# A gated-delta-rule sequence kernel on one core: the order of masks, value convolutions and triangular solves around the end of an iteration

## What is computed

```
mixed = hidden @ W_qkv.T                 # 2048 channels: 512 queries, 512 keys, 1024 values
mixed = silu(causal_conv(mixed, 4 taps)) # each channel by itself
beta  = sigmoid(hidden @ W_b.T);  g = -exp(A_log) * softplus(hidden @ W_a.T + dt_bias)
for t in tokens:                         # 16 heads of 64, state S is 64 x 64
    S = S * exp(g_t);  delta = (v_t - S^T k_t) * beta_t
    S = S + k_t delta^T;  o_t = S^T q_t
out = (rmsnorm(o * silu(hidden @ W_z.T)) * norm_weight) @ W_out.T
```

## Time and profile before

| | us |
|---|---|
| median of 3 runs (lowest, highest) | 1509.21 (1507.35, 1512.29) |
| the profiled execution's own time | 1500.96 |
| its span | 1499.0 |
| PE busy in the span | 1280.1 |
| DVE busy | 908.4 |
| ACT busy | 702.4 |
| POOL busy | 313.7 |

### The profile page before, as it was taken

The page is one execution under the profiler, slowest core; times in us unless marked ns, Lnnn a source line. Parts: engine busy times, 40 slices in busy tenths (PEclk is TensorE's granted clock), DMA queues, the critical chain, the costliest instruction groups (busy, mean ns, idle before and its releaser), DMA issues.

```text
span 1499.0 us, 26935 instructions
## 1 busy us (share of the span) xinstructions
PE 1280.1 (85%) x11040; PEld 926.5 (62%) x11048; DVE 908.4 (61%) x2349; ACT 702.4 (47%) x1353; POOL 313.7 (21%) x234
## 2 busy tenths in 40 slices
PE   3668799788879888889986859998899989989898
PEld 2355668567566766767765536665567656666566
DVE  4897987988798887969155333543436423463321
ACT  1657365564746556482451324424452344523442
POOL 5122352515235151523320010000100000000000
PEclk9768978796897889787898788999999999999999
DMA  4000000000000000010220000000000000000000
GB/s 126 4 2 5 1 2 11 2 12 2 11 1 2 12 2 8 2 33 8 74 86 8 1 1 0 1 8 2 8 0 8 1 2 8 0 1 1 1 8 7
DMA packets 15066, 17.69 MB, mean 12 GB/s; under 512 B 2567, under 2 KB 13216, under 8 KB 14560
## 3 DMA queue, kind: packets, MB, share of 16 engines
q1 hardware_dynamic: 12768, 14.09, 2.9%
q0 software_dynamic: 576, 1.76, 0.4%
q10 hardware_dynamic: 1600, 0.12, 0.1%
HBM read 13.87 MB, written 2.10 MB: 11 GB/s over the span
## 4 chain that ended last, share of the span: by engine, by line
PE 60%; DVE 24%; ACT 10%; issue 3%; POOL 2%; DMA 1%; SPq 0%; DVEq 0%; ACTq 0%
PE ps L1564 8%; PE ps L1554 8%; PE ps L1352 6%; DVE arena L1905 4%; PE ps L1118 4%; PE ps L1262 3%; DVE arena L1908 3%; PE ps L1194 3%; ACT arena L1003 2%; DVE arena L2177 2%; PE ps L1249 2%; PE ps L1656 2%; PE ps L1103 2%; PE ps L1620 2%; DVE arena L1822 2%
## 5 line engine op out<-in xcount | busy, mean ns | idle before, releaser
L1822 DVE SCALAR_TENSOR_TENSOR arena<-ps,conv_w,arena 128x255 f32<-128x255 f32 (+2 forms) x384 | 163.3, 475 | 16.4 <-ACT arena L671 11.8
L965 ACT ACTIVATE arena<-ps 128x512 f32<-128x512 f32 x144 | 85.3, 597 | 180.6 <-PE ps L1554 180.6
L537 POOL TENSOR_TENSOR rstd<-var_eps,half_power 128x2 f32<-128x2 f32 (+1 forms) x28 | 23.3, 834 | 608.7 <-DVE var_eps L1793 608.6
L1564 PEld LDWEIGHTS ps<-arena 128*128 128x128 f32 x1152 | 132.6, 192 | 24.8 <-issue 9.9
L1564 PE MATMUL ps<-arena 128*128 128x128 f32 x1152 | 136.9, 277 | 7.1 <-ACT arena L965 4.1
L1554 PE MATMUL ps<-arena 128*128 128x512 f32 x288 | 134.2, 612 | 0.0
L2148 DVE SCALAR_TENSOR_TENSOR arena<-ps,gates,arena 128x128 f32<-128x128 f32 x128 | 36.0, 343 | 113.8 <-PE ps L1564 113.5
L531 POOL TENSOR_SCALAR arena<-arena 32x1024 f32<-32x1024 f32 x32 | 88.5, 2765 | 53.4 <-DVE arena L1917 51.4
L1905 DVE TENSOR_TENSOR arena<-arena 128x30 f32<-128x30 f32 (+14 forms) x240 | 95.2, 396 | 7.3
L2214 DVE TENSOR_REDUCE arena<-ps 128x8 f32<-128x2048 f32 (+1 forms) x24 | 54.8, 2292 | 63.1 <-PE ps L1620 63.1
L1554 PEld LDWEIGHTS ps<-arena 128*128 128x128 f32 x288 | 51.4, 194 | 60.9 <-issue 45.2
(11 more groups left out here) (246 smaller groups left out, 2830.3 us busy)
## 6 DMA issues: line engine op xcount, KB each, us to landing
arena<-in_routed_up SPq DMA_DIRECT2D x1, 2048.0 KB, 10.2
arena<-in_routed_down SPq DMA_DIRECT2D x1, 2048.0 KB, 14.7
x_ln<-in_x SPq DMA_DIRECT2D x8, 128.0 KB, 2.3
arena<-in_w_mix SPq DMA_DIRECT2D x1, 1024.0 KB, 11.0
x_in<-in_x SPq DMA_DIRECT2D x8, 128.0 KB, 2.4
out_x<-x_res SPq DMA_DIRECT2D x8, 128.0 KB, 1.9
arena<-out_x SPq DMA_DIRECT2D x4, 256.0 KB, 2.8
out_x<-arena SPq DMA_DIRECT2D x4, 256.0 KB, 2.2
```

Of the source, the lines that this page charges most:

```text
L965: act.activation(hid1[half][:, i, :], ps[:, banks[i], :], ACT.Gelu).then_inc(s["mgelu"], 1)
L1564: mm = pe.matmul(ps[:, bank, c * P:(c + 1) * P], hid1[half][:, i, c * P:(c + 1) * P], m_down[:, e, i, :], start=(i == 0), stop=(i == HT1 - 1))
L1822: ins = dve.scalar_tensor_tensor(conv_tile(f, m)[:, sh:SEQ], ps[:, PAIR_BANK[p], j * SEQ:(j + 1) * SEQ - sh], conv_w[:, m, TAPS - 1 - sh:T ...
```

## The change

The pairs 5, 6 and 7 move from banks 4, 2, 4 to banks 1, 2, 2, so that banks 3 and 4 are free once queries and keys are convolved. Batches 0 and 1 both use the first couple of banks of `KK_BANKS` and batch 2 the second (`pair_of`). Products 0, 1 and 2 move on DVE from the start of the next iteration to between the convolutions of the values: pairs 0 to 5, product 0, pair 6, products 1 and 2, pair 7. With them move the keys, sums, decays and silus on PE and ACT, and masks 0 and 1 on POOL ahead of unit blocks 2 and 3. In the next iteration `turn_norm` and `beta_decay` come later on PE, and DVE's remaining products 3 to 7 are spread between the parts of `prepare`, `exponents` and `log_decays`. No instruction is added or taken away. In order on PE, from `solve32` on: sum 0, merge32 twice, pair 5, solve64 twice, first solve_and_merge64, key 0, second solve_and_merge64, pair 6, merge64, sum 1, key 1, merge64, sum 2, pair 7, key 2.

```diff
...
 INV_STEPS = 2 * BLOCK - 2
-PAIR_BANK = (0, 1, 3, 4, 2, 4, 2, 4)
+PAIR_BANK = (0, 1, 3, 4, 2, 1, 2, 2)
...
+def pair_of(k):
+    return max(k - 1, 0) % 2
 def over_heads(ap, n):
...
             normalise(i, 1)
-        if has_n:
-            pool.wait_ge(s["gm_ready"], CH * NB * (n + 1))
+        if has_f:
+            masked_decays(f, 0)
+            masked_decays(f, 1)
+        if has_n:
+            pool.wait_ge(s["gm_ready"], CH * NB * (n + 1) + (2 if has_f else 0))
             after(pool, "hn_ready", CH * (i + 1))
...
             pool.wait_ge(s["ln_rstd"], 1)
-        if has_f:
-            masked_decays(f, 0)
-            masked_decays(f, 1)
-            pool.wait_ge(s["gm_ready"], CH * NB * f + 2)
         if has_n:
...
         i, n, f = it, it + 1, it + 2
-        if has_f:
-            turned_norm(f)
         if has_n:
...
             turned_heads(i - 1, 1, 0)
-        if has_f:
-            exponentials(f)
         if has_n:
             decay_matrix(n, 4)
+        if has_f:
+            turned_norm(f)
         if has_i and i > 0:
...
             decay_matrix(n, 5)
+        if has_f:
+            exponentials(f)
+        if has_n:
             chunk_ends(n)
...
             merged32(n, 0)
+        if has_f:
+            silu(f, 0)
+        if has_n:
             merged32(n, 1)
             solved64(n, 0, 0)
+        if has_f:
+            seed(f, 5)
+            silu(f, 1)
+        if has_n:
             solved64(n, 0, 1)
...
         if has_f:
-            seed(f, 5)
+            silu(f, 2)
+            silu(f, 3)
         if has_n:
...
         if has_f:
-            seed(f, 6)
-            silu(f, 0)
+            decay_matrix(f, 0)
         if has_n:
...
         if has_f:
-            seed(f, 7)
-            silu(f, 1)
+            seed(f, 6)
         if has_n:
...
         if has_f:
-            silu(f, 2)
+            decay_matrix(f, 1)
         if has_n:
...
         if has_f:
-            silu(f, 3)
-            decay_matrix(f, 0)
-            decay_matrix(f, 1)
             decay_matrix(f, 2)
+            seed(f, 7)
     turned_heads(SEQS - 1, 1, 0)
...
         pe.wait_ge(s["d_h_ready"], f + 1)
-        after(pe, "conv_done", NP * f - 1)
+        after(pe, "conv_done", NP * f)
         for c in range(CH):
...
         if p >= 5:
-            pe.wait_ge(s["conv_done"], NP * f + p - 1)
+            pe.wait_ge(s["conv_done"], NP * f + (1, 4, 6)[p - 5] + 1)
         elif not has_n:
...
-            pe.wait_ge(s["conv_done"], NP * n + k + 1)
+            pe.wait_ge(s["conv_done"], NP * n + (0, 5)[k] + 1)
         else:
...
             pe.wait_ge(s["qk_silu"], QK_TILES * (n + 1))
-            pe.wait_ge(s["conv_done"], NP * (n + 1))
-        elif k == 1:
+        elif k == 2:
...
-            pe.wait_ge(s["pt_ready"], CH * NB * n + k - 1)
+            pe.wait_ge(s["pt_ready"], CH * NB * n + max(k - 1, 1))
         for g in range(2):
             r = DH * g
-            mm = pe.matmul(ps[:, KK_BANKS[k % 2][g], 0:2 * P].rearrange("p (q n) -> p q n", q=2),
+            mm = pe.matmul(ps[:, KK_BANKS[pair_of(k)][g], 0:2 * P].rearrange("p (q n) -> p q n", q=2),
                            mix_qk[n % 2][r:r + DH, QK_TILES + b, cs], mix_qk[n % 2][r:r + DH, b::QK_TILES, cs],
...
         i, n, f = it, it + 1, it + 2
-        if has_f:
-            turn_norm(f)
         if has_n:
             decay_sums(n, 3)
-        if has_f:
-            beta_decay(f)
         if has_i and i > 0:
...
         if has_n:
+            key_products(n, 3)
             decay_sums(n, 4)
-            key_products(n, 3)
+        if has_f:
+            turn_norm(f)
         if has_i and i > 0:
...
         if has_n:
+            key_products(n, 4)
+        if has_f:
+            beta_decay(f)
+        if has_n:
             decay_sums(n, 5)
-            key_products(n, 4)
+            key_products(n, 5)
             chunk_ends(n, f, has_f)
             decay_sums(n, 6)
-            key_products(n, 5)
             decay_sums(n, 7)
...
             solve32(i, n, 1, has_i)
+        if has_f:
+            decay_sums(f, 0)
+        if has_n:
             merge32(n, 0)
             merge32(n, 1)
+        if has_f:
+            project(f, 5, n, has_n)
+        if has_n:
             solve64(i, n, 0, has_i)
...
             turn_first(0)
-        if has_f:
-            decay_sums(f, 0)
-            project(f, 5, n, has_n)
         if has_n:
             solve_and_merge64(n, 0)
+        if has_f:
+            key_products(f, 0)
         if it == SEQS - 2:
...
             up_tile(0, 0)
-        if has_f:
-            decay_sums(f, 1)
+        if has_n:
+            solve_and_merge64(n, 1)
+        if has_f:
             project(f, 6, n, has_n)
-        if has_n:
-            solve_and_merge64(n, 1)
         if it == SEQS - 2:
...
             up_tile(0, 1)
-        if has_f:
-            project(f, 7, n, has_n)
         if has_n:
             merge64(n, 0)
+        if has_f:
+            decay_sums(f, 1)
+            key_products(f, 1)
         if it == SEQS - 2:
...
         if has_f:
-            key_products(f, 0)
-            key_products(f, 1)
             decay_sums(f, 2)
+            project(f, 7, n, has_n)
             key_products(f, 2)
...
         dve.wait_ge(s["dm_ready"], CH * NB * n + k + 1)
-        if k == 0:
-            after(dve, "a64_psum", 4 * n)
-        lo, hi = KK_BANKS[k % 2]
+        if b == 0:
+            after(dve, "a64_psum", 4 * (n - 1) + 2 * (c + 1))
+        lo, hi = KK_BANKS[pair_of(k)]
         qk = ps[:, lo:hi + 1, 0:2 * P].rearrange("p g (q n) -> p g q n", q=2)
...
         if has_n:
-            products(me, n, 0)
+            products(me, n, 3)
         if has_f:
...
         if has_n:
-            products(me, n, 1)
-            products(me, n, 2)
+            products(me, n, 4)
         if has_f:
...
         if has_n:
-            products(me, n, 3)
+            products(me, n, 5)
         if has_f:
...
         if has_n:
-            products(me, n, 4)
+            products(me, n, 6)
         if has_f:
...
         if has_n:
-            products(me, n, 5)
+            products(me, n, 7)
         if has_f:
             log_decays(me, f, 2)
-        if has_n:
-            products(me, n, 6)
-            products(me, n, 7)
         if it == SEQS - 1:
...
         if has_f:
-            for p in range(2, NP):
+            for p in range(2, 6):
                 convolve(me, f, p)
+            products(me, f, 0)
+            convolve(me, f, 6)
+            products(me, f, 1)
+            products(me, f, 2)
+            convolve(me, f, 7)
     residual(SEQS - 1, 1)
...
```

More of the change, by code:

```diff
@@ L1460, in _ @@
                     up_tile(0, 0)
-                if has_f:
-                    decay_sums(f, 1)
-                    project(f, 6, n, has_n)
                 if has_n:
                     solve_and_merge64(n, 1)
+                if has_f:
+                    project(f, 6, n, has_n)
                 if it == SEQS - 2:
```

## The result

| | before | changed |
|---|---|---|
| median, us | 1508.28 | 1566.28 |
| ratio to before, 95% interval | | 1.040 [1.0364, 1.0436] |
| span of the profiled execution | 1499.0 | 1561.7 |
| DVE busy | 908.4 | 915.9 |
| PE's granted clock, mean | 0.891 | 0.867 |

A forecast was written before the change was run, and what follows sets the result against it. DVE, spine of a chain through all engines, was taken to bound the kernel by its waits between pair 0 and the inverse: 10.0 us against 7.03, +2.9 per stretch, +17.4 over six, total +17.6, so 1526 us, range 1500 to 1540.

The forecast's parts named there:

- First step: PE from pair 0's convolution: sum 0 waits for it, with all solves queued behind; net delay about 2 us.
- Second and third: DVE among the value convolutions: product 0 waits 3.5 us for decay 0, pair 6 0.75, product 2 1.5 for key 2.
- Fourth: Next iteration: turn_norm waits for prepare, key 4 queued behind; products 4, 5, 6 wait 1.85, 0.75, 1.15 us.
- Rival (c): PE idle 3.2 us ahead of turn_norm drops its clock to half for work behind; +24, 1533 us, chance 0.23.
- Rival (a): Decay 0 is ready when pair 5 ends, so waits shrink; iteration 2.2 us shorter, 1496 us, chance 0.17.
- Rival (b): DVE's waits are moved, not made; iteration within 0.7 us of before, say 1510 us, chance 0.18.

The follow-up runs named there:

- e6_decay0_late: e5_prepare_sum0 with decay 0 moved behind seed 6 on ACT and product 0 behind pair 6 on DVE: 1530.72 us, ratio 1.0177.
- e3_warm: The changed kernel with four added matmuls per iteration on PE ahead of turn_norm, results overwritten: 1539.62 us, ratio 1.0239.
- e1_sum0_late: The changed kernel with sum 0 put back behind the two merge32 on PE: 1552.44 us, ratio 1.0325.
- e4_prepare_early: The changed kernel with the next sequence's two prepare parts moved among the convolutions, ahead of products 0 and 1: 1520.24 us, ratio 1.0099.
- e5_prepare_sum0: The changed kernel with the edits of e4_prepare_early and e1_sum0_late together: 1492.95 us, ratio 0.9912.
- e2_masks_first: The changed kernel with masks 5 to 7 made ahead of the inverse root of the norm on POOL: 1557.07 us, ratio 1.0361.

## Why the prediction was wrong in size

**The bound and the view were right.** DVE is the spine and the loss is DVE's waiting in the stretch from pair 0 to the inverse. The places of the waits were the ones forecast. The times, for T = 398.02, in us after T:

| start of | forecast | measured | behind by |
|---|---|---|---|
| product 0 | 19.55 | 21.0 | 1.4 |
| product 2 | 26.85 | 28.3 | 1.5 |
| turn_norm | 33.4 | 36.0 | 2.6 |
| product 4 | 35.15 | 38.8 | 3.6 |
| product 5 | 37.9 | 43.1 | 5.2 |
| product 6 | 41.1 | 46.6 | 5.5 |
| inverse | 47.5 | 53.0 | 5.5 |

**First step: right in kind, short by 1.4.** Sum 0 waited for pair 0 and all solves moved. The prediction took half clock only "up to T + 13.6", as before; it lasted to T + 18.8, so key 0 and the first solve_and_merge64 had half the speed that I gave them.

**Second and third: right.** DVE waited 4.3 us for decay 0 where I had 3.5, 0.6 for seed 6 (0.75), 1.55 for key 2 (1.5). A reading that came later, in the expectation for e6_decay0_late, that decay 0 was too early on ACT, fell with that run.

**Fourth: this is the step that failed.** It priced PE behind `turn_norm` at full clock: turned heads, key 4, `beta_decay`, sum 5 and key 5 ran at a granted clock of 0.50. Between `turn_norm` and product 5 the measured times fall back by another 2.6 us (2.6 behind, then 5.2), and the waits at products 4 and 5 are 2.80 and 2.62 us where the step had 1.85 and 0.75. The idle time ahead of `turn_norm` was forecast at 3.2 us and measured 4.34. e3_warm shows that this clock is worth 27 us, nearly half of the 58.

Rival (c) had this mechanism, with a chance of 0.23, and its price for it in the stretch, 6.6 - 3.8 = 2.8 us, was about right. Its 50.4 fell short of the 53.6 measured because it kept the other terms of the forecast, and its 40.85 for the inverse that follows because it took for granted that a fall in one stretch spares the next. The kernel before did that by turns; in the changed one no inverse took less than 42.0, and their mean is 43.6.

**What was missing altogether:** the h_tok instructions, 0.59 us for the pair before and 1.78 here. I costed `prepare` at its old duration in a new neighbourhood. In the table that is the step from 1.5 to 2.6 us behind. So of the 5.5 us of this stretch 1.5 come from the half clock in the first step, 1.1 from h_tok and 2.9 from behind `turn_norm`.

**The sum.** It was one iteration's order, worked out at the old clock, times six: +2.9 us a stretch where +9.0 was measured, and nothing for the inverses, which grew by 0.9 each. The repairs of e1_sum0_late and e4_prepare_early take 14 and 46 us off, and both keep the change's idea: masks between the convolutions, the values through banks 1 and 2. The largest single loss was `prepare` behind pair 7 with `turn_norm` needing it, an order that the fourth step names and priced too low. Rival (a), that the overlap works, is out for this order. Its 1496 is close to the 1493 of e5_prepare_sum0, but that is no support for it: it wanted 2.2 us off an iteration by shorter waits in the stretch, and there only 0.3 came off, the rest in the inverses. Rival (b) is out by the interval.

## What to carry to other kernels

A price taken from a stretch holds only with the clock and the neighbours that the stretch had. Where a reordering leaves PE idle for some us, price the work behind the gap at half clock as the first case, and test it by filling the gap with matmuls that nobody reads. When a stage is moved, look at what then precedes it in a queue that must not run dry: here moving 1.5 us of normalisation to a better place gave 46. And where added matmuls raise the clock in one stretch, look for the half clock in the next before counting the gain.

## What the runs showed of the hardware

DVE's normalisation of 128x128 fp32 (SBUF to SBUF, two scalars per partition) takes 0.34 us, and 0.78 and 1.08 beside POOL's 128x512 products. One such case, from the timeline of the changed kernel:
```profile
431.88 1.03 POOL L506 TENSOR_TENSOR arena<-con,log_decay 128x512 f32<-128x512 f32 x1
432.21 0.78 DVE L1812 TENSOR_SCALAR h_tok<-x_ln,mv,rstd 128x128 f32<-128x128 f32 x1
```
It ends 0.08 us behind POOL's instruction. The Trainium skill (GPSIMD Engine Reference, 1. Specifications) says that POOL shares its SBUF interfaces with VectorE and contends with some of its instructions, those in a 2-port mode or with two SBUF inputs. This trace agrees in so far as h_tok is slowed, and is back at 0.34 us in e2_masks_first with the masks moved away, while DVE's products, which read PSUM and SBUF, kept their 0.68 us beside the same masks. That h_tok runs in a 2-port mode no trace here shows.
